# A routed feed-forward layer on one core: the order of slot tiles, routing visits and table payload

## The chip, the cores and the metric

The kernel is one program on one core of a Trainium2 chip. Its time is device microseconds of one launch. Below, TensorE multiplies, VectorE (DVE), ScalarE (ACT) and GpSimd (POOL) compute and copy, and SyncE (SP) issues transfers.

## The reference

`x` has 4 x 1024 tokens of 512 float32 numbers, and each of the 4 batches names one of 64 categories. With `t` = 4096 tokens, 8 experts and room for 512 tokens in each:

```
h = x @ cond_W[cat] + cond_b[cat]                 # conditioning, per batch
probs = softmax(h @ Wr);  eidx = argmax(probs);  p = probs[eidx]
rank = number of earlier tokens with the same eidx
keep = rank < 512;  slot (eidx, rank) gets the token
per expert: y = relu(h[slots] @ W1[e]) @ W2[e] * p        # W1 512x2048, W2 2048x512
out = x + y scattered to its tokens (a dropped token gets x alone)
```

## The kernel before, in words

The program is written by hand, one instruction list per engine. Each engine works its list in order; semaphores tie the lists together. There is no planner: what stands earlier in a list runs earlier.

Matrix products keep float32 accuracy by splitting each operand into a high part (ScalarE copies it to fp32r) and a low part (VectorE subtracts the high part from the raw value), and adding three products, high x high, high x low and low x high.

*Conditioning and routing.* The tokens are 32 tiles of 128, four to a chunk. `cond_tile` multiplies a tile in 12 matmuls of 512 columns into one of three rotating PSUM banks, and VectorE's `store_h` adds the bias, which frees the bank. At the third k-block of a chunk's first tile TensorE waits for the second half of the chunk's low split. Chunks of x and blocks of the conditioning weight are split on ScalarE and VectorE at the tiles that `SPLIT_X` and `SPLIT_W` name; an entry of `SPLIT_X` holds the tiles of a chunk's first and second half. On a batch of eight tiles routing works in visits that TensorE makes between tiles, at tile numbers in lists by batch: `m_turn` (M_TURN: conditioning weight times router weight, by the transposed weight), copied on ScalarE and transposed on VectorE by `copy_m` (M_SUM); `route` (ROUTE: 64 matmuls of 128 columns with a weight of 32 columns: the logits), copied on ScalarE; `choose` on VectorE (CHOOSE: one-hot choice, counts of the tiles before); `rank_of` on TensorE and `place` on VectorE (both at PLACE: probability, its three-part float16 payload, `packed` = one-hot x payload, rank of each token, eight one-hot `select` rows); `fill_table` (FILL: 32 matmuls of packed x select, which add up the slot tables). At one tile the order on TensorE is turn, fill, rank, route; on VectorE store, choose, copy_m, place, splits.

GpSimd stores finished chunks of h to memory (`store_chunk`); the last 8 tiles are stored one by one by SyncE. When the table is complete, `gather_early` fetches rows of expert 0 from memory. Rows of the last 4 tiles (`late`) are added by a one-hot product of three bfloat16 parts. Then the first quarter of expert 0 is multiplied directly, and from there on the loop's scheme holds.

*The experts.* A step is one quarter of one expert: 128 x 4 hidden columns by 512 slots. The first product of a quarter is done by a seven-product scheme (P1 to P7, each two pairs of six matmuls of 256 columns), from sums of blocks of W1 (`sum_w1`: four GpSimd additions) and of x (`sum_x`). The second product (`second_product(i, q, s)`: 12 matmuls of 512 columns for one of four slot tiles s) runs one step behind the first. TensorE's step is: first_and_fifth, slot tile 0, second_and_sixth, slot tile 1, seventh_and_third, slot tile 2, fourth, slot tile 3. ScalarE makes the hidden tiles (`relu`, high part) behind the third and fourth products, VectorE their low parts (`hidden_lo`); slot tile 0 of the next step waits for all four. VectorE also makes low parts of W1, W2 and x, and scales finished outputs (`finish(i, s)`) behind slot tile s of a quarter that ends an expert. Once an expert, four VectorE transposes (`transpose_chunk`) turn the gathered rows between two steps; GpSimd gathers and scatters rows.

The loop covers experts 0 to 6 (28 steps); two steps of the last expert and its last second product follow.

## Time and profile before

| what | value |
|---|---|
| median of 3 runs | 798.09 us (797.9 to 798.27) |
| the profiled execution | 797.76 us, of which span 796.1 us |
| granted TensorE clock, mean | 0.999 of full speed |
| TensorE busy | 789.6 us, 99% of the span |
| VectorE, ScalarE, GpSimd busy | 581.2, 351.8, 517.2 us |
| chain of waits, share of TensorE | 98% |

The span is the time from the first to the last instruction; the profiled execution's own time is 1.7 us longer. Durations are of that one execution. In a timeline a matmul's length has some 0.16 us of latency in it, so lengths overlap; the rate is read from one start to the next. "xN" is a run of N alike.

### The profile page before, as it was taken

The numbers are of one execution on the slowest core, as the hardware profiler recorded it, in microseconds if no ns is written. First come the engines' busy times: TensorE is split into PE (matmuls) and PEld (weight loads), VectorE is DVE, ScalarE is ACT, GpSimd is POOL, SyncE is SP. The second block draws the span as 40 slices with busy tenths as digits, with TensorE's granted clock in tenths as the row PEclk, the third lists the DMA queues.
The fourth block names the chain that finished last, engine by engine and source line by source line (L and its number), as shares of the span: only waits on it lengthen the run. The fifth ranks groups of instructions, "written<-read, shape, count | busy, mean of one in ns | idle before, by whom it ended". The sixth has DMA issues, their size and how long they took to land.

```text
span 796.1 us, 14205 instructions
## 1 busy us (share of the span) xinstructions
PE 789.6 (99%) x5255; PEld 702.3 (88%) x5255; DVE 581.2 (73%) x764; ACT 351.8 (44%) x537; POOL 517.2 (65%) x392
## 2 busy tenths in 40 slices
PE   9999999999999999999999999999999999999997
PEld 6778789899999999999999999999999999999996
DVE  5678969799757886689657965797578767895532
ACT  4322246536443544455444544454445344544420
POOL 1000148898887688768878688768876888663601
PEclk9999999999999999999999999999999999999999
DMA  8988543542554154424553444435441544254201
GB/s 285 376 309 296 205 167 132 185 159 96 170 178 146 54 191 165 163 105 175 170 171 109 168 162 149 154 129 172 172 144 58 185 157 142 103 188 176 71 1 54
DMA packets 61103, 127.20 MB, mean 160 GB/s; under 512 B 8310, under 2 KB 8310, under 8 KB 60562
## 3 DMA queue, kind: packets, MB, share of 16 engines
q1 hardware_dynamic: 47714, 95.19, 34.4%
q0 software_dynamic: 13216, 31.38, 12.2%
q8 instruction: 17, 0.28, 0.1%
q10 hardware_dynamic: 144, 0.26, 0.1%
q14 instruction: 12, 0.10, 0.0%
HBM read 110.13 MB, written 25.17 MB: 170 GB/s over the span
## 4 chain that ended last, share of the span: by engine, by line
PE 98%; DMA 1%; SPq 0%; issue 0%; POOL 0%; DVE 0%; ACT 0%; POOLq 0%
PE y_ps L1500 44%; PE acc_ps L1398 20%; PE tp_ps L1398 19%; PE acc_ps L1316 6%; PE tp_ps L1316 3%; PE tp_ps L1247 1%; PE acc_ps L1412 1%; PE tp_ps L1412 1%; DMA stage<-cond_w 1%; PE y_ps L1232 0%; PE y_ps L1365 0%; PE acc_ps L1297 0%; PE y_ps L1316 0%; PE y_ps L1268 0%; PE y_ps L1374 0%
## 5 line engine op out<-in xcount | busy, mean ns | idle before, releaser
L1500 PE MATMUL y_ps<-w_split,xt_split 128*128 128x512 f32 x1536 | 371.1, 391 | 0.0
L1500 PEld LDWEIGHTS y_ps<-w_split,xt_split 128*128 128x128 f32 x1536 | 280.7, 188 | 53.2
L1398 PE MATMUL acc_ps<-x_split,w_split 128*128 128x256 f32 x1320 | 181.1, 283 | 0.0
L1398 PEld LDWEIGHTS acc_ps<-x_split,w_split 128*128 128x128 f32 x1320 | 172.1, 191 | 5.0 <-DVE w_split L956 0.2
L1398 PE MATMUL tp_ps<-x_split,w_split 128*128 128x256 f32 x1284 | 176.4, 283 | 0.0
L967 DVE TENSOR_TENSOR w_split<-stage,w_split 128x1024 fp32r<-128x1024 f32 x64 | 113.1, 1807 | 80.8 <-ACT w_split L671 80.8
L1398 PEld LDWEIGHTS tp_ps<-x_split,w_split 128*128 128x128 f32 x1284 | 167.6, 191 | 4.9 <-ACT logits_t L730 0.2
L546 POOL DMA_INDIRECT rows<-h_rows,idx_all x112 | 133.7, 1194 | 32.9 <-issue 32.3
L664 ACT ACTIVATE w_split<-stage 128x1024 fp32r<-128x1024 f32 x64 | 54.0, 843 | 97.8 <-PE acc_ps L1398 46.0
L503 POOL TENSOR_TENSOR w_sums<-stage 128x512 f32<-128x512 f32 x31 | 42.9, 1385 | 67.1 <-DVE w_split L956 60.1
L956 DVE TENSOR_TENSOR w_split<-stage,w_split 128x1024 fp32r<-128x1024 f32 x64 | 73.5, 1148 | 15.7 <-ACT w_split L664 15.6
L956 DVE TENSOR_TENSOR w_split<-w_sums,w_split 128x1024 fp32r<-128x1024 f32 x62 | 77.7, 1255 | 5.6 <-ACT w_split L664 5.4
L733 ACT ACTIVATE xt_split<-tp_ps 128x512 fp32r<-128x512 f32 x64 | 38.0, 598 | 79.7 <-PE tp_ps L1398 77.8
L562 POOL DMA_INDIRECT out<-rows,put_all x32 | 37.6, 1176 | 52.4 <-DVE rows L1090 44.9
L733 ACT ACTIVATE xt_split<-acc_ps 128x512 fp32r<-128x512 f32 x64 | 38.0, 598 | 68.9 <-PE acc_ps L1398 67.1
L664 ACT ACTIVATE w_split<-w_sums 128x1024 fp32r<-128x1024 f32 x62 | 65.1, 1049 | 5.4 <-POOL w_sums L506 4.9
L671 ACT ACTIVATE w_split<-stage 128x1024 fp32r<-128x1024 f32 x64 | 64.3, 1060 | 0.0
L1067 DVE SCALAR_TENSOR_TENSOR xt_split<-tp_ps,xt_split 128x512 fp32r<-128x512 f32 x64 | 44.0, 691 | 26.4 <-ACT xt_split L733 25.9
L1067 DVE SCALAR_TENSOR_TENSOR xt_split<-acc_ps,xt_split 128x512 fp32r<-128x512 f32 x64 | 43.8, 687 | 22.5 <-ACT xt_split L733 21.3
L508 POOL TENSOR_TENSOR w_sums<-stage 128x512 f32<-128x512 f32 x31 | 59.8, 1927 | 0.0
L496 POOL DMA_DIRECT2D h_rows<-rows x6 | 4.8, 797 | 80.4 <-DVE rows L867 80.4
L506 POOL TENSOR_TENSOR w_sums<-w_sums,stage 128x512 f32<-128x512 f32 x31 | 53.9, 1738 | 2.4
(183 smaller groups left out, 802.4 us busy)
## 6 DMA issues: line engine op xcount, KB each, us to landing
stage<-w SPq DMA_DIRECT2D x64, 1024.0 KB, 7.3
b_rows<-x SPq DMA_DIRECT2D x8, 1024.0 KB, 9.4
h_rows<-rows POOLq DMA_DIRECT2D x6, 1024.0 KB, 9.1
stage<-cond_wt SPq DMA_DIRECT2D x4, 1024.0 KB
x_more<-x_t SPq DMA_DIRECT2D x4, 1024.0 KB, 9.1
stage<-x_t SPq DMA_DIRECT2D x3, 1024.0 KB, 7.6
stage<-cond_w SPq DMA_DIRECT2D x3, 1024.0 KB, 9.6
h_rows<-rows SPq DMA_DIRECT2D x8, 256.0 KB, 2.4
```

Source lines behind the costliest of these rows:

```text
L506: nc.gpsimd.tensor_tensor(w1_sum(1), w1_sum(0), w1_raw(0, 0, slot), ALU.subtract).then_inc(s_comb, 1)
L508: nc.gpsimd.tensor_tensor(w1_sum(2), w1_raw(0, 0, slot), w1_raw(1, 0, slot), ALU.subtract).then_inc(s_comb, 1)
L546: pool.indirect_dma_start(out=h_quart[:, t * P:(t + 1) * P], out_offset=None, in_=h_parts, in_offset=bass.IndirectOffsetOnAxis(ap=idx_all[ ...
L664: nc.scalar.activation(split_part(w1s, grp, HI), w1_group(grp, slot), ACTF.Copy).then_inc(s_w1hi, 1)
L671: nc.scalar.activation(w2s[:, slot, HI, ks, :], stage[:, 2 + slot, ks, :], ACTF.Copy).then_inc(s_w2hi, 1)
L733: nc.scalar.activation(hts[:, (u % 2) * QF + tile, HI, :], (upper(u) + lower(u))[tile], ACTF.Relu).then_inc(s_hhi, 1)
L956: nc.vector.tensor_tensor(split_part(w1s, grp, LO), w1_group(grp, (u + 1) % 2), split_part(w1s, grp, HI).bitcast(f32), ALU.subtract).then_ ...
L967: nc.vector.tensor_tensor(w2s[:, slot, LO, ks, :], stage[:, 2 + slot, ks, :], w2s[:, slot, HI, ks, :].bitcast(f32), ALU.subtract).then_inc ...
L1067: nc.vector.scalar_tensor_tensor(hts[:, at, LO, :], (upper(u) + lower(u))[tile], 0.0, hts[:, at, HI, :].bitcast(f32), ALU.max, ALU.subtrac ...
L1316: last = nc.tensor.matmul(cond_bank(n), xts[:, c % 4, a, k, t * P:(t + 1) * P], w2s[:, (c // CPB) % 2, w, k, :], start=(k == 0 and (a, w) ...
L1398: last = nc.tensor.matmul(out, w1s[wg][:, w, wb, k, f], xes[xg][:, a, xb, k, :], start=start and k == 0 and (w, a) == (HI, HI), stop=True, ...
L1500: last = nc.tensor.matmul(y_ps[:, s, :], hts[:, (q % 2) * QF + jj, a, s * P:(s + 1) * P], w2s[:, q % 2, w, jj, :], start=(first and jj == ...
```

## The change

Four things. In the loop TensorE does slot tiles 2 and 3 of the second product one after the other, and fourth behind them; VectorE's list in a step is reordered to go with it. The payload and `packed` are made by GpSimd (`pack`) from the probability that VectorE leaves. The tile lists of routing are changed: turn, fill and route stand at seven tiles instead of ten, and copy_m is ahead of choose at one tile. In the head, the second conditioning block's high part is halved between ScalarE and VectorE as the first already was; some loads of SyncE change places; and the first two of the four sums of W1's second quarter are done ahead of the wait for the late parts.

```diff
...
     M_TURN = [4, 8, 13, 18]
-    M_SUM = [5, 10, 13, 18]
-    ROUTE = [6, 11, 15, 20]
-    CHOOSE = [8, 13, 18, 22]
-    PLACE = [10, 15, 20, 24]
+    M_SUM = [5, 9, 14, 19]
+    ROUTE = [8, 13, 18, 20]
+    CHOOSE = [9, 14, 19, 22]
+    PLACE = [11, 16, 21, 24]
     FILL = [13, 18, 23, 27]
...
     KEEP_FIRST = 12
+    HALVED = 2
+    PAY_STEPS = 5
     LATE = 4
...
         rest = sb("rest", [P, TPB], f32)
+        scaled = sb("scaled", [P, TPB], f32)
         payload = sb("payload", [P, NT, Q], f16)
...
         s_oh = sem("onehot_done")
+        s_prob = sem("prob_done")
+        s_pay = sem("payload_steps_done")
+        s_pack = sem("packed_done")
         s_rank = sem("rank_done")
...
 
+            load_cond(2)
             load_next_xt(4)
-            load_cond(2)
             load_next_xt(5)
...
             load_cond_wt(2)
+            sp.wait_ge(s_turn, 3)
+            load_cond_wt(3)
             load_next_xt(6)
...
             load_cond(3)
-            sp.wait_ge(s_turn, 3)
-            load_cond_wt(3)
 
...
             def sum_w1(g):
+                first_sums(g)
+                second_sums(g)
+
+            def first_sums(g):
                 slot = g % 2
...
                                         ).then_inc(s_comb, 1)
+
+            def second_sums(g):
+                slot = g % 2
                 nc.gpsimd.tensor_tensor(w1_sum(2), w1_raw(0, 0, slot), w1_raw(1, 0, slot), ALU.subtract
...
 
+            def pack(b):
+                tiles = slice(TPB * b, TPB * (b + 1))
+                done = PAY_STEPS * b
+                pool.wait_ge(s_mask, 15)
+                pool.wait_ge(s_prob, b + 1)
+                nc.gpsimd.tensor_copy(payload[:, tiles, 1], prob[:, :]).then_inc(s_pay, 1)
+                pool.wait_ge(s_pay, done + 1)
+                nc.gpsimd.tensor_tensor(rest[:, :], prob[:, :], payload[:, tiles, 1], ALU.subtract).then_inc(s_pay, 1)
+                pool.wait_ge(s_pay, done + 2)
+                nc.gpsimd.tensor_scalar(scaled[:, :], rest[:, :], LOWER, None, ALU.mult).then_inc(s_pay, 1)
+                pool.wait_ge(s_pay, done + 3)
+                nc.gpsimd.tensor_copy(payload[:, tiles, 2], scaled[:, :]).then_inc(s_pay, 1)
+                pool.wait_ge(s_pay, done + 4)
+                nc.gpsimd.tensor_tensor(payload[:, tiles, 3], scaled[:, :], payload[:, tiles, 2], ALU.subtract
+                                        ).then_inc(s_pay, 1)
+                pool.wait_ge(s_pay, done + 5)
+                pool.wait_ge(s_oh, b + 1)
+                if b >= 1:
+                    pool.wait_ge(s_tab, b)
+                nc.gpsimd.tensor_tensor(packed[:, :, :, :],
+                                        onehot.unsqueeze(3).to_broadcast([P, TPB, E, Q]),
+                                        payload[:, tiles, :].unsqueeze(2).to_broadcast([P, TPB, E, Q]),
+                                        ALU.mult).then_inc(s_pack, 1)
+
             for c in range(NCH - 2):
+                for b in range(BATCH):
+                    if TPC * c <= PLACE[b] < TPC * (c + 1):
+                        pack(b)
                 store_chunk(c)
+            pack(BATCH - 1)
 
...
             gather_early()
+            first_sums(1)
             pool.wait_ge(s_part[2], LATE)
-            sum_w1(1)
+            second_sums(1)
             pool.wait_ge(s_hlast, 16 * LATE)
...
                     act.wait_ge(s_acc, TPC * CPB * (b - 1))
-                cols = slice(0, CH // 2 if (b, k) == (0, 0) else CH)
+                cols = slice(0, CH // 2 if b == 0 and k < HALVED else CH)
                 nc.scalar.activation(w2s[:, b % 2, HI, k, cols], stage[:, 1, k, cols], ACTF.Copy
...
                     dve.wait_ge(s_rank, b)
+                    dve.wait_ge(s_pack, b)
                 then(nc.vector.tensor_tensor(onehot, score[:, :, :], wide(best[:, :]), ALU.is_equal))
...
                 then(nc.vector.tensor_reduce(total[:, :], expo[:, :, :], AX.X, ALU.add))
-                then(nc.vector.reciprocal(prob[:, :], total[:, :]))
-                then(nc.vector.tensor_copy(payload[:, tiles, 1], prob[:, :]))
-                then(nc.vector.tensor_tensor(rest[:, :], prob[:, :], payload[:, tiles, 1], ALU.subtract))
-                then(nc.vector.tensor_scalar(payload[:, tiles, 2], rest[:, :], LOWER, None, ALU.mult))
-                then(nc.vector.scalar_tensor_tensor(payload[:, tiles, 3], rest[:, :], LOWER, payload[:, tiles, 2],
-                                                    ALU.mult, ALU.subtract))
+                if b >= 1:
+                    dve.wait_ge(s_pay, PAY_STEPS * b)
+                nc.vector.reciprocal(prob[:, :], total[:, :]).then_inc(s_prob, 1)
                 if b >= 1:
                     dve.wait_ge(s_tab, b)
-                nc.vector.tensor_tensor(packed[:, :, :, :],
-                                        onehot.unsqueeze(3).to_broadcast([P, TPB, E, Q]),
-                                        payload[:, tiles, :].unsqueeze(2).to_broadcast([P, TPB, E, Q]),
-                                        ALU.mult)
                 dve.wait_ge(s_rank, b + 1)
...
             dve.wait_ge(s_mask, 15)
-            def first_half():
-                dve.wait_ge(s_w0[0], 16)
-                nc.vector.tensor_copy(w2s[:, 0, HI, 0, CH // 2:], stage[:, 1, 0, CH // 2:]).then_inc(s_whalf, 1)
-                dve.wait_ge(s_whalf, 1)
+            def second_half(k):
+                dve.wait_ge(s_w0[k], 16)
+                nc.vector.tensor_copy(w2s[:, 0, HI, k, CH // 2:], stage[:, 1, k, CH // 2:]).then_inc(s_whalf, 1)
+                dve.wait_ge(s_whalf, k + 1)
 
...
                 split_first(k)
-                if k == 0:
-                    first_half()
+                if k < HALVED:
+                    second_half(k)
                 split_cond(0, k)
...
                 store_h(n // TPC, n % TPC)
+                if n in M_SUM:
+                    copy_m(M_SUM.index(n))
                 if n in CHOOSE:
                     choose(CHOOSE.index(n))
-                if n in M_SUM:
-                    copy_m(M_SUM.index(n))
                 if n in PLACE:
...
                 new, done = u == QN - 1 and not last, u == QN
-                for half in range(2):
-                    split_w2(i, u, half)
+                if not done:
+                    split_w2(i, u, 0)
+                    split_w2(i, u, 1)
                 add_fifths(i, u)
...
                     finish(i, 0)
+                    split_w2(i, u, 0)
                 if not last:
...
                     finish(i, 2)
+                    split_w2(i, u, 1)
+                    finish(i, 3)
                 hidden_lo(i, u, 2)
...
                     split_x(i, 3)
-                if done:
-                    finish(i, 3)
 
...
                 pe.wait_ge(s_sel, b + 1)
+                pe.wait_ge(s_pack, b + 1)
                 for t in range(TPB):
...
                             pe.wait_ge(s_whi, k + 1)
+                            if k < HALVED:
+                                pe.wait_ge(s_whalf, k + 1)
                         elif w == LO:
...
             keep_warm(KEEP_FIRST)
-            pe.wait_ge(s_whalf, 1)
             first_tiles()
...
 
-            def step(i, u):
+            def step(i, u, last=False):
                 first_and_fifth(i, u)
...
                 second_product(i, u - 1, 2)
-                fourth(i, u)
-                second_product(i, u - 1, 3)
+                if last:
+                    fourth(i, u)
+                    second_product(i, u - 1, 3)
+                else:
+                    second_product(i, u - 1, 3)
+                    fourth(i, u)
 
...
             for u in range(2, QN):
-                step(E - 1, u)
+                step(E - 1, u, u == QN - 1)
             for s in range(SB):
...
```

## Rows read from the trace of the kernel before

**Rows 1.** The page, part 1: busy us, share of the span, instructions.
```profile
PE 789.6 (99%) x5255; PEld 702.3 (88%) x5255; DVE 581.2 (73%) x764; ACT 351.8 (44%) x537; POOL 517.2 (65%) x392
```

**Rows 2.** Chain of waits, the loop's last steps: start us, length us, what.
```profile
755.27 1.43 PE tp_ps L1398 x12
756.70 2.75 PE y_ps L1500 x12
759.45 2.87 PE acc_ps L1398 x24
...
777.74 13.64 PE y_ps L1500 x60
```

**Rows 3.** Timeline of TensorE, conditioning stage: start, length, line, names, shape, count.
```profile
29.23 3.01 PE L1316 MATMUL tp_ps<-w_split,xt_split 128*128 128x512 f32 x12
32.08 2.88 PE L1316 MATMUL acc_ps<-w_split,xt_split 128*128 128x512 f32 x12
34.89 1.08 PE L1232 MATMUL y_ps<-stage,wr 128*32 128x128 f32 x32
...
41.54 3.01 PE L1316 MATMUL acc_ps<-w_split,xt_split 128*128 128x512 f32 x12
44.48 1.96 PE L1247 MATMUL tp_ps<-x_more,m 128*32 128x128 f32 x64
...
102.39 5.61 PE L1316 MATMUL acc_ps<-w_split,xt_split 128*128 128x512 f32 x24
107.84 2.89 PE L1316 MATMUL tp_ps<-w_split,xt_split 128*128 128x512 f32 x12
```

**Rows 4.** Timeline of ScalarE, head; in brackets its idle time and the releaser.
```profile
5.37 0.42 ACT L633 ACTIVATE w_split<-stage 128x256 fp32r<-128x256 f32 x1 [0.99 <-DMA stage<-cond_w]
...
8.42 0.63 ACT L633 ACTIVATE w_split<-stage 128x512 fp32r<-128x512 f32 x1 [1.54 <-DMA stage<-cond_w]
```

**Rows 5.** The page, part 6: transfers by line, KB each, us to landing.
```profile
stage<-cond_w SPq DMA_DIRECT2D x3, 1024.0 KB, 9.6
```

**Rows 6.** Timeline of VectorE, routing.
```profile
52.74 0.43 DVE L877 STREAM_TRANSPOSE by_tok<-logits_t 128x256 f32<-128x256 f32 x1
...
55.38 0.31 DVE L856 STREAM_TRANSPOSE m<-m_rows 128x128 f32<-128x128 f32 x1
...
56.54 0.69 DVE L867 TENSOR_TENSOR rows<-acc_ps,b_rows 128x512 f32<-128x512 f32 x1 [0.28 <-PE acc_ps L1316]
57.15 1.22 DVE L837 TENSOR_TENSOR xt_split<-stage,xt_split 128x1024 fp32r<-128x1024 f32 x1
...
77.88 0.18 DVE L907 CAST payload<-prob 128x8 f16<-128x8 f32 x1
...
79.06 0.22 DVE L919 TENSOR_TENSOR ranks<-y_ps,chosen 128x64 f32<-128x64 f32 x1
...
79.57 2.19 DVE L924 TENSOR_SCALAR select<-iota_c,place_all 128x512 f16<-128x512 f16 x8
```

**Rows 7.** Timeline of GpSimd, early gather and sums.
```profile
102.63 1.10 POOL L532 DMA_INDIRECT early_rows<-h_rows,tok_all  x1 [11.30 <-DMA h_rows<-rows]
...
118.57 1.76 POOL L511 TENSOR_TENSOR w_sums<-stage,w_sums 128x512 f32<-128x512 f32 x1
```

**Rows 8.** Timeline of VectorE, splits of the first hidden input.
```profile
119.09 1.78 DVE L1050 TENSOR_TENSOR x_split<-turned,x_split 128x512 fp32r<-128x512 f32 x1
```

**Rows 9.** Timeline of TensorE, end of the first quarter and one loop step.
```profile
127.56 3.33 PE L1398 MATMUL acc_ps<-x_split,w_split 128*128 128x256 f32 x24
...
254.32 3.04 PE L1398 MATMUL acc_ps<-x_split,w_split 128*128 128x256 f32 x24
```

**Rows 10.** Timeline of VectorE, around two step ends of the loop.
```profile
253.70 4.13 DVE L1073 STREAM_TRANSPOSE turned<-rows 128x512 f32<-128x512 f32 x4
...
272.73 1.41 DVE L1067 SCALAR_TENSOR_TENSOR xt_split<-acc_ps,xt_split 128x512 fp32r<-128x512 f32 x2
...
280.15 4.48 DVE L967 TENSOR_TENSOR w_split<-stage,w_split 128x1024 fp32r<-128x1024 f32 x2
```

## The prediction

> **What bounds the kernel now.** I read the page's engine table first, then the chain of waits, then each engine's timeline. The table has TensorE busy for 99% of the span [rows 1], and its chain is 98% TensorE. So only two things move the time: a change in how long TensorE's own stream lasts, and a wait put into it or taken out. An edit on VectorE, ScalarE or GpSimd counts only where TensorE waits for it.
>
> In the loop over experts a step is seven groups of twelve narrow matmuls (256 columns) and four of twelve wide ones (512). The chain has them end to end: 1.43 us for twelve narrow and 2.87 for 24 behind wide ones, 2.75 for twelve wide between narrow ones [rows 2]. Four times 2.75 and seven times 1.435 are the 21.04 us of a step; nothing is left for waits. The sixty wide ones at the end take 13.64, or 2.73 a dozen, so an entry into a wide group costs 0.02 and one into a narrow group gives 0.01 back.
>
> In the conditioning stage two tiles without a visit take 5.45 (102.39 to 107.84) [rows 3], 2.725 each. A tile behind a routing visit takes 2.85, one ahead of a visit 2.81 (29.23, 32.08, 34.89): a visit costs 0.12 + 0.09 = 0.21 beside its own matmuls. Between the rank matmuls and route(1) the tile takes 2.94 (41.54 to 44.48), so a rank visit of its own costs about 0.13.
>
> **The sum, part by part** (us, minus is faster).
>
> *Halved second block.* ScalarE's 0.63 us split of the second conditioning block starts when the load lands, and TensorE waits for it [rows 4]. Half the columns take 0.42 (at 5.37) and save 0.21; VectorE, idle there, does the rest. **-0.2** (-0.3 to +0.1, if VectorE gets there last).
>
> *Visits.* Turn, route and fill stand at 4, 6, 8, 11, 13, 15, 18, 20, 23, 27 now and at 4, 8, 13, 18, 20, 23, 27 afterwards: three fewer, 3 x 0.21 = 0.63. Turn(1) is no longer alone and ranks no longer precede a route (about 0.3 less), while ranks alone go from two tiles to four (2 x 0.13 more). **-0.65** (-0.3 to -0.9). Turn(1) now comes at about 32.5 instead of 34.89 and needs a load issued at 21.8, just behind the wait for turn(0); a load of that kind lands 9.6 after issue [rows 5], at 31.4, so I take nothing and keep +0.4 as a bound. SyncE issues cond_w(2) before x_t(4) now, which does not wait for route(0); the third turning load and x_t(6), x_t(7), cond_w(3) go out together near 50 to 55 and four of them need some 12 us, so cond_w(3) lands near 65. ScalarE waits for it at tile 16 and VectorE's stores are some tiles behind, but TensorE needs that weight only at tile 24: nothing.
>
> *The second half of chunk 4.* Its low split stays at tile 14, and choose(1) now comes to tile 14 too, ahead of it on VectorE. Count from the start of tile 14: its end 2.85, the store starts 0.2 behind, 0.61 to the next instruction (56.54 to 57.15) [rows 6], copy_m(2) 0.24, choose 2.64 (52.74 to 55.38), the split 1.22: done at 7.8. TensorE is through tile 15 at 5.58 and asks for that half after six matmuls of tile 16, at 6.94. Before, choose was at tile 13 and the split done four tiles' time earlier. **+0.9** (0 to +1.0). This wait eats the visits' gain.
>
> *Choosing and placing later, payload on GpSimd.* The payload instructions leave VectorE: 1.18 us a batch (77.88 to 79.06), so place is 3.1 instead of 4.3 with its eight selects of 2.1 together. GpSimd gets five chained small instructions and one of 256 elements; its nearest row is 1.3 to 1.8 for 512 elements [rows 7], so I estimate 2.3 a batch, bounds 1.5 to 5. It starts when prob is there, 1.3 us behind the rank tile, and fill comes 5.6 us behind it: 4.3 us of cover. GpSimd has nothing else then but storing a chunk; chunk 2's store goes 3 to 4 us later, and VectorE needs its buffer 14 us later. At 5 us a fill would wait 0.7 twice. For batch 3 VectorE is tight: from the end of tile 21 store, place(2), both splits of chunk 6, store and choose(3) are 0.2 + 0.6 + 3.1 + 2.3 + 0.6 + 2.4 = 9.2; TensorE reaches rank(3) after 9.1. **+0.2** (0 to +1.3). From there VectorE runs about 2 us behind its old times, into tile 27.
>
> For the upper bound the row is this: a 512-element VectorE split with both inputs in SBUF took 1.78 at 119.09 [rows 8] and ended 0.5 us behind GpSimd's sum that began at 118.57, where the same form takes 0.69 otherwise. The Trainium skill ("SBUF — State Buffer", Who interferes with whom) has it that such an instruction, or a VectorE one in a two-port mode, and a GpSimd instruction lock each other out for a whole instruction. By that rule pack and the selects would block each other, up to an instruction's length, and rank(3) would come later by that much; the trace agrees for the sums (1.78 against 0.69), and no row of before shows GpSimd beside the selects.
>
> *Early rows.* The gather waits for tile 27's row store to land: its first issue is at 102.63 [rows 7]. Tile 27's store on VectorE is some 1.8 us late, so the gather is at 104.5. TensorE arrives at 111.0; the third of four gathers lands at 111 to 112 and is asked for at 111.9. **+0.1** (0 to +1.0).
>
> *First two sums of W1(1) ahead of the wait.* They now run beside VectorE's last remainders, which set the end of the late rows; one blocked instruction there is up to 0.7. **+0.2** (0 to +0.8). In return, of the four sums beside the first x splits only two are left, and the blocked 1.8 us (the 1.78 row, and one of 1.39 before it) goes. TensorE's first 24 narrow matmuls in that stretch took 3.33 where 24 take 2.87 [rows 2, 9], and some 0.3 more is lost beside them; a wait for the copies of the new pair, 0.2, is next. **-0.5** (-0.7 to 0).
>
> *Loop.* Slot tiles 2 and 3 side by side, and fourth beside the next step's first group, remove one wide and one narrow entry a step: 0.02 - 0.01 = 0.015, for 29 steps **-0.4** (-0.5 to 0). The Trainium skill ("TensorE: Matmul & The Clock Gate", Back-to-back issue gap) gives the isolated gap as a function of the columns alone; by that this edit is worth nothing, and the sum comes out 0.4 higher. The trace differs by the 0.02 above.
>
> What it costs: fourth now ends with the step, and the next product's slot 0 needs hidden tile 3, which was 5.6 us behind fourth and is now 2.9. In the step that starts at 254.32 [rows 9] fourth ends at 272.6; VectorE's pair of hidden tiles, 1.41 us, starts at 272.73 and is done at 274.14 [rows 10]. Shifted by the 2.7 of the product that went ahead, it is done 1.5 us into the next step: 1.3 to spare. finish(3) and the split of W2 are moved so that VectorE is free by then. **0**.
>
> Sum: -0.2 - 0.65 + 0.9 + 0.2 + 0.1 + 0.2 - 0.5 - 0.4 = **-0.35**. The profiled execution took 797.76 (span 796.1, 1.7 around it), so it would take 797.4. The median of the runs is 0.33 above it: **797.8**.
>
> **Rivals.**
> A, slower: *the transposes come late.* Once an expert, four transposes (4.13 at 253.70) follow the last W1 split of a step, which now ends 2.7 later. They then run from 2.1 to 6.3 us into the step; two W2 splits follow, 3.5 to 4.5 us (the latter is the 4.48 row), then an addition of 0.4 that the seventh product wants at 11.25. That is 10.2 to 11.2 against 11.25. GpSimd's x sums run beside it as well; if they block VectorE for one more instruction (1.1 us, the 1.78 row), TensorE waits up to 1 us in seven experts, and knock-on waits for sums and copies come on top: about 0.4 a time is 2.8, 800.6. It decides from a pair of splits above 4.5 us. Against it: such a pair takes at most 4.48 in the trace.
> B, faster: *the wait at tile 16 is not there or hides another.* The sum without it is -1.25; with all small costs at nothing, -1.75: 796.3 to 796.8. For it: little but my counting of one VectorE queue, with 0.9 of 7.8 us over.
> C: *GpSimd and VectorE block each other in routing.* Rank(3), the table and the early gather each late by most of their bounds: +1.5 on the sum, 799.3.
> D: *the adjacency gives nothing* and visits half: about +0.7, 798.5; still no measurable change.
>
> **How the numbers follow.** A measurement of this kernel tells some 0.2%, 1.6 us, from no change: 796.5 to 799.7. Forecast (with D) 0.60, A 0.12, B 0.16, C 0.12. A is slower, C a third of its cases, B nearly all faster than the bound or at it. That makes 0.17 faster, 0.65 same, 0.18 slower. The range takes the forecast's own bounds and half of A, B and C: 796.3 to 799.9.
>
> **What would show it.** A gap in TensorE's stream of 0.7 to 1.0 at tile 16 behind six matmuls, released by VectorE's split of chunk 4, and choose(1) just ahead of that split; seven clusters of small matmuls in place of ten; steps of 21.02 instead of 21.04, with 24 wide in 5.47; the first narrow matmuls behind the first quarter with at most 0.3 of gaps; the early gather's first issue near 104.5. The forecast fails if steps of the loop are longer than 21.04, if a fill waits for pack, or if tile 16 starts clean.

## The result, and the profile after

The changed kernel took 801.94 us in the median of 6 runs (801.63 to 803.34), against 798.12 for the kernel before (6 runs, 797.9 to 798.28). The ratio is 1.0054 [1.0044, 1.0064]: half a percent slower, and outside the predicted range of 796.3 to 799.9. The profiled execution took 801.63 us, 3.87 more than the one before; its span is 799.7. Two of the six, at 803.12 and 803.34, had a mean granted clock of 0.996 where the other four had 0.999, and took 1.4 more than these. Neither was profiled, so no row shows where the clock fell.

The page's engine table (busy us, share, instructions), which answers to [rows 1]:

```profile
PE 789.6 (99%) x5255; PEld 702.5 (88%) x5255; DVE 586.7 (73%) x745; ACT 350.3 (44%) x537; POOL 539.7 (67%) x416
```

TensorE's busy time is what it was. All 3.6 us of the longer span are gaps. The chain of waits says that they aren't in the loop (start us, length us, what), answering to [rows 2]:

```profile
142.59 10.91 PE y_ps L1540 x48
...
756.17 5.47 PE y_ps L1540 x24
763.07 2.88 PE acc_ps L1438 x24
...
781.37 13.64 PE y_ps L1540 x60
```

The 24 wide matmuls stand side by side. The x48 piece is the end of the first quarter's stretch and the start of the steady loop; x60 is its end. They lie 638.78 us apart, and 639.36 in the trace before, where x48 starts at 138.38: the loop gained 0.58. x48 itself starts 4.21 later. TensorE's timeline shows why (start, length, engine, line, operation, count; in brackets idle time and releaser):

```profile
60.41 1.67 PE L1357 MATMUL tp_ps<-w_split,xt_split 128*128 128x512 f32 x6 [0.67 <-DVE xt_split L879]
...
87.53 3.04 PE L1357 MATMUL acc_ps<-w_split,xt_split 128*128 128x512 f32 x12
90.78 0.20 PE L1295 MATMUL y_ps<-chosen,before 128*128 128x64 bf16 x1 [0.21 <-DVE prior L939]
...
99.70 0.63 PE L1307 MATMUL y_ps<-select,packed 128*32 128x128 f16 x32 [0.41 <-DVE select L960]
...
102.31 0.33 PE L1319 MATMUL y_ps<-ident,slots 128*128 128x128 f32 x1 [0.98 <-ACT slots L694]
...
104.56 6.00 PE L1357 MATMUL acc_ps<-w_split,xt_split 128*128 128x512 f32 x24
...
113.12 1.72 PE L1414 MATMUL y_ps<-ident,early_rows 128*128 128x128 f32 x12
...
118.93 1.30 PE L1405 MATMUL y_ps<-late_sel,late_parts 128*128 128x128 bf16 x18 [1.47 <-DVE late_parts L986]
120.07 0.26 PE L1367 MATMUL tp_ps<-tok_n,spread_w 128*128 128x32 f16 x4
...
131.83 3.04 PE L1438 MATMUL acc_ps<-x_split,w_split 128*128 128x256 f32 x24
```

Five waits in brackets, and 24 matmuls that take 6.00, where the kernel before had no wait between the head and the first quarter. With the same points read from the trace before, the loss adds up (us; a wait costs its idle time and 0.1 to 0.5 more):

| point | before | after | later by | lost since the point above |
|---|---|---|---|---|
| tile 4 (end of the head) | 17.49 | 17.37 | -0.12 | -0.12 |
| tile 24 | 87.52 | 87.53 | 0.01 | +0.13: the wait at tile 16, less what the visits save |
| fill(3) | 98.84 | 99.70 | 0.86 | +0.85: ranks of batch 3, last selects |
| the table's matmul | 100.20 | 102.31 | 2.11 | +1.25: slots |
| early rows | 110.56 | 113.12 | 2.56 | +0.45: 24 matmuls of tiles 29 and 30 in 6.00, before 5.61 [rows 3] |
| spread | 115.62 | 120.07 | 4.45 | +1.89: late parts |
| x48 | 138.38 | 142.59 | 4.21 | -0.24: 3.04 for the 3.33 of [rows 9] |
| x60 | 777.74 | 781.37 | 3.63 | -0.58: the loop |

Who holds up VectorE stands in the timelines of GpSimd and of VectorE, after (GpSimd first):

```profile
91.94 0.81 POOL L502 DMA_DIRECT2D h_rows<-rows  x1 [7.08 <-DVE rows L909]
95.02 0.19 POOL L544 CAST payload<-prob 128x8 f16<-128x8 f32 x1 [2.26 <-DVE prob L951]
...
96.62 0.62 POOL L558 TENSOR_TENSOR packed<-chosen,payload 128x256 f16<-128x256 bf16 x1
97.17 1.81 POOL L609 MEMSET early_rows<- 128x2048 f32 x1
106.38 1.15 POOL L573 DMA_INDIRECT early_rows<-h_rows,tok_all  x1 [7.40 <-DMA h_rows<-rows]
...
111.77 1.29 POOL L513 TENSOR_TENSOR w_sums<-stage 128x512 f32<-128x512 f32 x1
113.14 1.62 POOL L516 TENSOR_TENSOR w_sums<-w_sums,stage 128x512 f32<-128x512 f32 x1
```

```profile
95.27 4.38 DVE L960 TENSOR_SCALAR select<-iota_c,place_all 128x512 f16<-128x512 f16 x8
...
111.20 2.42 DVE L986 TENSOR_TENSOR late_parts<-late_rest,late_parts 128x512 bf16<-128x512 f32 x1
113.54 1.77 DVE L980 TENSOR_TENSOR late_rest<-rows,late_parts 128x512 f32<-128x512 f32 x1
```

And one row of GpSimd's timeline in the kernel before that the prediction did not use:

```profile
89.51 1.83 POOL L568 MEMSET early_rows<- 128x2048 f32 x1
```

GpSimd clears the buffer of the early rows with one instruction. Before, it did so at 89.51, four microseconds ahead of the last selects. In the changed list this instruction stands behind `pack(BATCH - 1)`, which waits for a probability until 95.02. So it now runs beside the selects: they take 4.38 where [rows 6] has 2.19. Fill and the table wait for the selects, the stores of the last tiles follow, and the early gather leaves at 106.38 instead of 102.63 [rows 7]. GpSimd's next items, the two sums that the change moved ahead of the wait, start only at 111.77, exactly beside the last late parts, and hold two VectorE instructions of 0.69 for 2.42 and 1.77. TensorE waits for those.

For the 0.4 lost in tiles 29 and 30 the profile names no releaser, but TensorE's list does. Between the two tiles it waits for `s_win` and reads four addresses into registers (lines 1394 and 1395 of the kernel after). VectorE signals `s_win` when it has written `window_at`, a few instructions behind the copy of the table. From the timelines of VectorE and of TensorE's weight loads (PEld), before:

```profile
101.37 0.16 DVE L932 CAST window_at<-window 1x4 int32<-1x4 f32 x1
102.16 5.41 PEld L1316 LDWEIGHTS acc_ps<-w_split,xt_split 128*128 128x128 f32 x24
```

and after:

```profile
104.19 0.16 DVE L968 CAST window_at<-window 1x4 int32<-1x4 f32 x1
104.33 2.69 PEld L1357 LDWEIGHTS acc_ps<-w_split,xt_split 128*128 128x128 f32 x12
107.52 2.61 PEld L1357 LDWEIGHTS acc_ps<-w_split,xt_split 128*128 128x128 f32 x12 [0.51 <-issue]
```

Before, `window_at` is there 0.63 ahead of tile 29's first weight load, and tile 30 follows without a gap. After, it comes only with that load. The 14 traces of this document fall into the same two groups: 0.63 or 0.64 ahead in five, and 5.61 for the two tiles; with the load or later in nine, and 0.4 to 0.7 lost up to the early rows. No run changes this wait alone, so the cause is argued from the list and the traces, not shown.

### The profile page after: what moved, and what is told of

Same layout as the page of the kernel before. It is cut to its first block, busy times and chain, and to the rows that moved or that the text cites. A ratio compares the mean times of both kernels' runs of the same rounds, so it can differ in the third digit from the quotient of the medians.

```text
span 799.7 us, 14227 instructions
## 1 busy us (share of the span) xinstructions
PE 789.6 (99%) x5255; PEld 702.5 (88%) x5255; DVE 586.7 (73%) x745; ACT 350.3 (44%) x537; POOL 539.7 (67%) x416
## 4 chain that ended last, share of the span: by engine, by line
PE 95%; DVE 3%; issue 2%; ACT 0%; POOL 0%; POOLq 0%
PE y_ps L1540 44%; PE acc_ps L1438 20%; PE tp_ps L1438 19%; PE acc_ps L1357 5%; PE tp_ps L1357 2%; PE tp_ps L1285 1%; PE acc_ps L1452 1%; PE tp_ps L1452 1%; PE acc_ps L1375 1%; PE acc_ps L1338 1%; PE y_ps L1270 0%; DVE late_parts L986 0%; DVE xt_split L879 0%; PE y_ps L1357 0%; DVE select L960 0%
## 5 line engine op out<-in xcount | busy, mean ns | idle before, releaser
L1540 PE MATMUL y_ps<-w_split,xt_split 128*128 128x512 f32 x1536 | 365.6, 391 | 0.0
L587 POOL DMA_INDIRECT rows<-h_rows,idx_all x112 | 137.7, 1229 | 33.0 <-issue 32.1
L1003 DVE TENSOR_TENSOR w_split<-stage,w_split 128x1024 fp32r<-128x1024 f32 x64 | 101.1, 1610 | 44.4 <-ACT w_split L713 44.4
L992 DVE TENSOR_TENSOR w_split<-w_sums,w_split 128x1024 fp32r<-128x1024 f32 x62 | 96.3, 1555 | 2.8 <-ACT w_split L706 2.8
L992 DVE TENSOR_TENSOR w_split<-stage,w_split 128x1024 fp32r<-128x1024 f32 x64 | 76.7, 1199 | 6.6 <-ACT w_split L706 6.4
L603 POOL DMA_INDIRECT out<-rows,put_all x32 | 42.8, 1336 | 51.7 <-DVE rows L1126 44.2
L513 POOL TENSOR_TENSOR w_sums<-stage 128x512 f32<-128x512 f32 x31 | 43.5, 1402 | 36.7 <-DVE w_split L992 36.3
L524 POOL TENSOR_TENSOR w_sums<-stage,w_sums 128x512 f32<-128x512 f32 x31 | 55.6, 1794 | 0.0
L521 POOL TENSOR_TENSOR w_sums<-stage 128x512 f32<-128x512 f32 x31 | 50.9, 1643 | 4.0 <-DVE late_parts L986 4.0
L516 POOL TENSOR_TENSOR w_sums<-w_sums,stage 128x512 f32<-128x512 f32 x31 | 51.7, 1669 | 2.4
```

The source lines that it names most:

```text
L516: nc.gpsimd.tensor_tensor(w1_sum(1), w1_sum(0), w1_raw(0, 0, slot), ALU.subtract).then_inc(s_comb, 1)
L524: nc.gpsimd.tensor_tensor(w1_sum(3), w1_raw(0, 1, slot), w1_sum(1), ALU.subtract).then_inc(s_comb, 1)
L587: pool.indirect_dma_start(out=h_quart[:, t * P:(t + 1) * P], out_offset=None, in_=h_parts, in_offset=bass.IndirectOffsetOnAxis(ap=idx_all[ ...
L992: nc.vector.tensor_tensor(split_part(w1s, grp, LO), w1_group(grp, (u + 1) % 2), split_part(w1s, grp, HI).bitcast(f32), ALU.subtract).then_ ...
L1003: nc.vector.tensor_tensor(w2s[:, slot, LO, ks, :], stage[:, 2 + slot, ks, :], w2s[:, slot, HI, ks, :].bitcast(f32), ALU.subtract).then_inc ...
L1540: last = nc.tensor.matmul(y_ps[:, s, :], hts[:, (q % 2) * QF + jj, a, s * P:(s + 1) * P], w2s[:, q % 2, w, jj, :], start=(first and jj == ...
```

## The experiments

My theory after this reading: two collisions on GpSimd, of about 1.7 us each, are nearly all of the miss, and payload on GpSimd as such is harmless. The rivals: the payload's own instructions are what costs, or the later tiles. In the expectations a run goes by its label: e1 to e7 are experiments 1 to 7, and e9 to e13 are experiments 8 to 12.

How the results are read: where TensorE reaches tile 4 differs from one execution to the next (17.27 to 18.66 over these traces, by when loads land). So beside the times each trace is given by its **middle**, from the start of tile 4 to the start of x48. It is 120.89 before and 125.22 after. It is read from one trace of each kernel, but stretches that two kernels have in common agree well: from tile 4 to tile 24 it is 70.14 to 70.16 in the kernel after and in experiments 1 to 3. The loop, x48 to x60, is 638.78 in each kernel that has the new order and 639.35 or 639.36 in each that hasn't.

**1. The clearing ahead of pack(3)** (after, otherwise unchanged).

```diff
+            pool.wait_ge(s_acc, NT - 8)
+            nc.gpsimd.memset(early_rows[:, :, :], 0.0).then_inc(s_zero, 1)
             pack(BATCH - 1)
-            pool.wait_ge(s_acc, NT - 8)
-            nc.gpsimd.memset(early_rows[:, :, :], 0.0).then_inc(s_zero, 1)
```

> The changed kernel with GpSimd's clearing of early_rows put ahead of pack(3) instead of behind it. Theory L (lock): the clearing, 1.81 us beside the last eight selects, blocks VectorE, which makes them 4.38 instead of 2.65. Moved away, the selects are back at 2.6 to 2.9, the waits of the last fill (0.41) and of the table (0.98) nearly go, the early gather starts near 104.6 instead of 106.4, and the time falls by 1.8 to 2.8, to 799.2 to 800.2. Theory Q (queue): VectorE is late by its order alone (two splits and place at tile 21), the clearing is a bystander; the selects stay above 4 and the time stays within 0.4 of 801.9.

The profiled execution took 800.01, 1.62 less than after's; middle 123.48, 1.74 less. The median of four is 801.33 (1.0043 [1.0026, 1.006]), outside the expected 799.2 to 800.2: the three other executions (800.83 to 801.94) had a granted clock of 0.996, as two of after's had. So by its times alone this run is weak. Experiments 2 and 3 differ by the same edit, over ten executions each with no clock under 0.998, and there it is worth 1.83 (800.01 to 798.18). From its timelines:

```profile
92.86 1.83 POOL L569 MEMSET early_rows<- 128x2048 f32 x1
```

```profile
95.36 2.66 DVE L960 TENSOR_SCALAR select<-iota_c,place_all 128x512 f16<-128x512 f16 x8
```

The waits of fill and table are gone. The selects take 2.66 beside pack and 2.19 without it, so pack costs them 0.47. The wait for the late parts remains whole.

**2. The two sums back behind the wait** (after, otherwise unchanged).

```diff
             gather_early()
-            first_sums(1)
             pool.wait_ge(s_part[2], LATE)
+            first_sums(1)
             second_sums(1)
```

> The changed kernel with the first two W1(1) sums of GpSimd back behind the wait for the late parts. Theory L: those two sums (1.29 and 1.62) block two VectorE instructions of the late rows (2.42 and 1.77 instead of 0.69 each); behind the wait both are 0.69, TensorE's wait of 1.47 for the late parts falls under 0.3, but the first x splits are blocked again (1.4 and 1.8 us instead of 0.7) and some 0.4 of waits returns near the first quarter's end: net 0.8 to 1.4 faster, 800.5 to 801.1. Theory Q: the late rows are late because tiles 27 to 30 are; the wait stays above 1 and the time within 0.4 of 801.9, or is slower by what the early sums gave.

800.01 (799.6 to 800.36, 10 runs), 1.0025 [1.0015, 1.0035]; middle 123.55, 1.67 less than after. Late parts take 0.69 each and TensorE's last wait is gone. The time is below the expected 800.5 to 801.1: up to the spread matmuls the edit gains 1.97, more than the wait of 1.47 shows, and 0.3 of it is lost again behind them. The selects' 4.39 and the waits at fill and table stay.

**3. Both.**

> Both edits, clearing ahead of pack(3) and all four sums behind the wait. Theory L: the two collisions were all of the excess over the forecast; left are the wait at tile 16 (0.7), rank(3) (0.2) and the gain of the loop and of the visits: 797.8 to 798.6. Theory Q: no better than 801.3.

798.18 (797.58 to 799.1, 10 runs), 1.0004 [0.9994, 1.0014]: no difference from before that can be told. The middle is 121.80, 3.42 less than after, and 1.74 + 1.67 is 3.41: the two collisions are independent and add up. What is left of waits in brackets behind the head are tile 16 and rank(3); tiles 29 and 30 still take 6.01.

**4. The loop's new order alone** (the kernel before with the change's edits of `step` and of VectorE's list in the loop).

```diff
+                if last:
+                    fourth(i, u)
+                    second_product(i, u - 1, 3)
+                else:
+                    second_product(i, u - 1, 3)
+                    fourth(i, u)
```

> The kernel before with the loop's part of the change alone: slot tiles 2 and 3 side by side, fourth last, VectorE's step reordered. By the chain, steps of 21.02 instead of 21.04, 29 of them, no waits: 0.4 to 0.7 faster than before, 797.4 to 797.7. If the reordered step only pays because the head runs late, or if rival A (late transposes) holds from this starting point, no gain or slower, 798.1 and up.

797.58 (796.98 to 798.3, 10 runs), 0.9995 [0.9985, 1.0005]. The time alone can't tell it from nothing; the trace can: loop 638.78 instead of 639.36, middle 120.87 as before.

**5. Experiment 3 with the second half of chunk 4 split a tile earlier.**

```diff
-    SPLIT_X = [None, None, (3, 4), (6, 7), (12, 14), (16, 17), (21, 21), (23, 25)]
+    SPLIT_X = [None, None, (3, 4), (6, 7), (12, 13), (16, 17), (21, 21), (23, 25)]
```

> The kernel of e3 (clearing first, sums behind) with chunk 4's second split at tile 13 instead of 14, ahead of choose(1). Theory: the wait at tile 16 (0.67 after six matmuls, 0.83 with what lies around it) goes and nothing later takes it, so TensorE is 0.8 earlier to the end: 797.3 to 797.5 where e3 took 798.2. Rival: VectorE's queue at tiles 21 to 24 is the bound there (rank(3) waits 0.2 for it already) and does not move with TensorE, so the gain is given back and the time stays at 798.1.

797.46 (796.65 to 798.07, 11 runs), 0.9992 [0.9983, 1.0001]; middle 120.83, 0.97 less than experiment 3. The wait at tile 16, shown as 0.67, is gone. It was one VectorE queue that was too long, by 0.7 as shown, where the prediction had counted 0.9.

**6. Payload and packed back on VectorE** (after, otherwise unchanged; `packed` signals `s_pack`, and the calls of `pack` are gone from GpSimd's list).

```diff
-                nc.vector.reciprocal(prob[:, :], total[:, :]).then_inc(s_prob, 1)
+                then(nc.vector.reciprocal(prob[:, :], total[:, :]))
+                then(nc.vector.tensor_copy(payload[:, tiles, 1], prob[:, :]))
...
+                nc.vector.tensor_tensor(packed[:, :, :, :],
...
+                                        ALU.mult).then_inc(s_pack, 1)
```

> The changed kernel with the payload and packed back on VectorE; tile lists, loop and early sums as changed. Theory L: GpSimd has no pack, so it clears early_rows near 92 to 94, and the selects are 2.19 instead of 2.65 to 4.38. VectorE gives 1.2 a batch for the payload and gets 0.5 (for the last batch 2.2) back; rank(3) waits 0.7 to 1.0 instead of 0.2 (its own 1.2 less 0.5), the last fill not more than that; the sums still block the late rows. 800.6 to 801.5 against 801.9. If the payload's own cover was worth its place: slower than 801.9.

801.49 (801.32 to 801.67, 4 runs), 1.0045 [1.003, 1.006]; middle 125.35, against 125.22. The clearing is ahead of the selects again (93.59) and they take 2.19, but VectorE's own 1.2 us a batch make rank(3) wait 1.03 and the table 0.71, and the collision with the sums is as it was (2.36 and 1.77). Taking the payload away from GpSimd doesn't save the kernel: it swaps one lateness for another. The middles differ by 0.13; by the times the two can't be told apart.

**7. The clearing beside the selects, in the kernel before.** This isolates the collision: one more wait holds GpSimd's clearing until the ranks of batch 3 are made. VectorE signals `s_ranks` ahead of its selects.

```diff
             pool.wait_ge(s_acc, NT - 8)
+            pool.wait_ge(s_ranks, BATCH)
             nc.gpsimd.memset(early_rows[:, :, :], 0.0).then_inc(s_zero, 1)
```

> The kernel before, with one thing changed: GpSimd's clearing waits until the last ranks are read, so it runs beside VectorE's last eight selects. Theory L: the selects take 3.8 to 4.0 instead of 2.19. VectorE has some slack here, since the last fill came 3.3 behind them: that fill does not wait; chunk 7's second split and tile 27's store come up to 1.7 later, the table may wait up to 0.3. Time 798.0 to 798.8. Theory Q (write-only clearing does not block VectorE): selects at 2.19 and the time of before, 797.9.

From the timelines of GpSimd and of VectorE:

```profile
93.94 1.81 POOL L570 MEMSET early_rows<- 128x2048 f32 x1 [4.05 <-DVEq L924]
```

```profile
93.90 3.83 DVE L927 TENSOR_SCALAR select<-iota_c,place_all 128x512 f16<-128x512 f16 x8
```

The selects take 1.64 longer beside a clearing of 1.81, with no pack in this kernel. TensorE has most of the slack here, though: no wait in brackets, 798.4 (798.25 to 798.81, 10 runs), 1.0007 [0.9997, 1.0016]; the middle is 121.27. Its 0.38 more is all in tiles 29 and 30, which take 5.99: `window_at` is late again. In the changed kernel the slack was already used up by the later tiles, so there the same collision cost 1.7. The Trainium skill ("SBUF — State Buffer", Who interferes with whom) says that a VectorE instruction in a two-port mode, which it lists `tensor_scalar` as able to enter, and one of GpSimd exclude each other for the whole instruction. Only for a VectorE instruction with two inputs in SBUF does it limit this to GpSimd instructions that read SBUF. 3.83 against 2.19 beside a clearing, which reads nothing, agrees; in which mode the selects run no view shows.

**8. Experiment 5 with chunk 6 split at tile 20**, ahead of place(2), so that VectorE is at choose(3) sooner.

```diff
-    SPLIT_X = [None, None, (3, 4), (6, 7), (12, 13), (16, 17), (21, 21), (23, 25)]
+    SPLIT_X = [None, None, (3, 4), (6, 7), (12, 13), (16, 17), (20, 20), (23, 25)]
```

> e5 with both splits of chunk 6 at tile 20 instead of 21, where VectorE idled 2.8 before tile 21's store. Theory: choose(3) comes 1.1 earlier, the 0.2 wait at rank(3) goes, VectorE is 1.1 ahead into tile 27, the early gather too: 0.2 faster than e5, 797.1 to 797.3. Rival: ScalarE's copy of the logits and its splits come too late at tile 20 and delay tile 21's store and place(2): the wait moves to a fill, and the time is that of e5 or up to 0.5 above.

796.49 (796.07 to 796.87, 11 runs), 0.9982 [0.9973, 0.9991]: the best version, and the interval is clear of the kernel before. The middle is 120.08, 0.75 less than experiment 5's; 0.38 more of the difference in span is the head. TensorE's timeline no longer has a wait behind its first matmul, and tiles 29 and 30 are back at 5.61:

```profile
101.35 5.61 PE L1357 MATMUL acc_ps<-w_split,xt_split 128*128 128x512 f32 x24
...
126.51 3.34 PE L1438 MATMUL acc_ps<-x_split,w_split 128*128 128x256 f32 x24
```

I had expected the rank wait of 0.2 alone to go, and 797.1 to 797.3. That wait was worth 0.36; the other 0.38 is in tiles 29 and 30, where `window_at` is 0.63 ahead again. The 3.34, for after's 3.04, is what the sums' return behind the wait gave back.

**9. The two sums in GpSimd's idle time before the gather** (experiment 8, the first two sums behind a wait for the copy of the slots).

```diff
+            pool.wait_ge(s_slots, 1)
+            first_sums(1)
             pool.wait_ge(s_zero, 1)
...
-            first_sums(1)
             second_sums(1)
```

> e9 with the first two W1(1) sums put where GpSimd waits for tile 27's row store: behind the copy of the slot tables (near 99.8), ahead of the early gather (102.5). Theory L: there VectorE has mostly PSUM reads; two of its instructions are blocked by up to 1 us, the early gather may be 0.3 late; the late rows stay at 0.69 each, and of the four sums beside the first x splits two are left, which takes back the 0.4 to 0.7 lost behind the first quarter (3.33 for 24 narrow becomes 2.9 to 3.0): 795.8 to 796.3. Rival: the block falls on tile 27's store and the table, so the gather starts 1 us later and TensorE waits for late or early rows: 796.5 to 797.3.

From the timelines of GpSimd, VectorE and TensorE:

```profile
99.62 1.29 POOL L513 TENSOR_TENSOR w_sums<-stage 128x512 f32<-128x512 f32 x1 [3.74 <-ACT slots L695]
100.99 1.29 POOL L516 TENSOR_TENSOR w_sums<-w_sums,stage 128x512 f32<-128x512 f32 x1
103.31 1.17 POOL L575 DMA_INDIRECT early_rows<-h_rows,tok_all  x1 [1.02 <-DMA h_rows<-rows]
```

```profile
101.03 1.30 DVE L1013 TENSOR_SCALAR tok_all<-tok_n 128x32 uint32<-128x32 f16 x1
102.42 0.16 DVE L969 CAST window_at<-window 1x4 int32<-1x4 f32 x1
```

```profile
105.45 3.01 PE L1358 MATMUL acc_ps<-w_split,xt_split 128*128 128x512 f32 x12 [0.42 <-issue]
```

797.13 (796.66 to 797.76, 11 runs), 0.9988 [0.9979, 0.9997]; middle 120.52, 0.44 more than experiment 8. Late parts are clean, and the x splits are too (24 narrow in 3.04 again), but the second sum now holds `tok_all`, one small VectorE instruction, for 1.30 instead of 0.18 (the stores take their usual 0.68). `window_at` stands behind it and comes 0.66 later than tile 29's first weight load, and tile 30 waits 0.42. The expectation was missed; the collision moved rather than went.

**10. The two sums ahead of the wait, in the kernel before.**

> The kernel before with one thing changed: the first two W1(1) sums ahead of the wait for the late parts. GpSimd is through the early gather at 107.7 there, so the sums run to about 110.6, when VectorE has a late part and a remainder of tile 30 and is past them before tile 31's store. Theory L with the position deciding: one instruction blocked, at most 0.3 on the late rows, and 0.5 gained behind the first quarter: 797.4 to 797.8. Rival: the early sums cost their collision wherever the gather ends, 1 us or more: 798.8 to 799.3.

From the timelines of GpSimd, VectorE and TensorE:

```profile
109.64 1.63 POOL L510 TENSOR_TENSOR w_sums<-w_sums,stage 128x512 f32<-128x512 f32 x1
```

```profile
109.18 0.93 DVE L958 TENSOR_TENSOR late_parts<-late_rest,late_parts 128x512 bf16<-128x512 f32 x1
110.04 1.78 DVE L952 TENSOR_TENSOR late_rest<-rows,late_parts 128x512 f32<-128x512 f32 x1
```

```profile
115.44 1.23 PE L1373 MATMUL y_ps<-late_sel,late_parts 128*128 128x128 bf16 x18 [0.53 <-DVE late_parts L958]
```

798.39 (798.19 to 799.18, 10 runs), 1.0004 [0.9995, 1.0014], between the two expectations. The middle is 121.58, 0.69 more than before, but most of that is not the edit's: 0.44 is lost ahead of tile 24, long before the sums, nearly all of it at the first route visit, where TensorE waits for a transposition that came late behind a load. From tile 24 to x48 it is 51.11 instead of 50.86, 0.25 more. So even with the gather on time this edit costs a little more (a TensorE wait of 0.53) than it gains. With the gather 3.7 late it costs 1.67 (experiment 2), with the gather 2.1 late 1.68 (experiment 1 against 3).

**11. Experiment 8 without the head's halving** (`HALVED = 1`).

> e9 with only the first conditioning block halved, as before. Theory: the second block's copy is 0.63 instead of 0.42 and TensorE waits for it: 0.2 slower than e9, 796.7. Rival: how late the block lands differs from execution to execution by more (TensorE's wait for it was 0.3, 0.6 and 1.1 in three traces with the same head), so nothing can be told: 796.3 to 796.7.

796.69 (796.38 to 797.54, 11 runs), 0.9982 [0.9973, 0.9991]; middle 120.06. In its trace tile 4 starts at 18.66, but that varies between 17.27 and 18.07 in nine traces with the halving and between 17.49 and 18.66 in five without. By the ratios to the kernel before, 0.9982 in both experiments, it is worth nothing that can be told. (Of the three waits that the expectation names, the 1.1 is experiment 4's and its head isn't halved.)

**12. Experiment 8 with payload and packed on VectorE.**

> e9 with the payload and packed on VectorE. Theory: with the collisions gone the question is only VectorE's own time: it does 1.18 more a batch and gets 0.46 back from the selects, so it is 0.7 later at rank(3), where e9 had some 0.9 to spare, and 1.4 later at tile 27; the early gather starts near 103.9: 0 to 0.5 slower than e9, 796.5 to 797.0. Rival: the payload on GpSimd is worth a microsecond by itself: 797.5.

797.95 (797.3 to 798.4, 11 runs), 0.9997 [0.9988, 1.0006]; middle 121.51, 1.43 more than experiment 8. From the timelines of TensorE and of VectorE:

```profile
86.95 0.63 PE L1310 MATMUL y_ps<-select,packed 128*32 128x128 f16 x32 [0.61 <-DVE select L963]
...
100.55 0.33 PE L1322 MATMUL y_ps<-ident,slots 128*128 128x128 f32 x1 [0.20 <-ACT slots L690]
```

```profile
95.69 2.19 DVE L963 TENSOR_SCALAR select<-iota_c,place_all 128x512 f16<-128x512 f16 x8
```

Both expectations were too low. Of the 1.43, 0.68 is lost ahead of tile 24, at the fill of batch 2, and some 0.4 each at the table and at tile 30 (5.98 for the two tiles). Payload on GpSimd, which the bare result seems to condemn, is worth about 1.4 us once the clearing is ahead of it; by the two ratios, 0.9997 and 0.9982, it is 1.2.

## Why the prediction was wrong

**The step that failed** is the term "choosing and placing later, payload on GpSimd, +0.2". It rested on the sentence "GpSimd has nothing else then but storing a chunk". That was true of the first three batches only. Behind pack(3), in unchanged lines of GpSimd's list, stood the clearing of the early rows. [rows 7] points at it: the 11.30 of idle time ahead of the early gather begin at 91.33, so GpSimd had worked until then, on the clearing. I had asked what pack itself costs and whom its result keeps waiting, not what is queued behind the instruction that waits. Rival C named the mechanism, GpSimd and VectorE blocking each other in routing, and the consequences (rank(3), table and early gather late), but priced it at +1.5 in all, from the bounds of terms that knew of pack alone. With a 1.8 us instruction in it this collision by itself was 1.74 (experiment 1); experiment 7 shows it without pack, as 1.64 on the selects.

**The second mis-sized term** is "first two sums ahead of the wait, +0.2 (0 to +0.8)". Taking it out gained 1.67 (experiment 2), and that is net of the 0.3 which the edit had gained behind it. I allowed for one blocked instruction of up to 0.7. There were two, lengthened by 1.73 and 1.08, and they were exposed because the gather, which is ahead of the sums in GpSimd's list, was late. This is no consequence of the first collision: with that one gone and the gather near its forecast time the sums still cost 1.68 (experiment 1 against 3), while in the kernel before, with the gather on time, they cost 0.25 net (experiment 10). The prediction had the later gather in one term and did not carry it into this one. "In return -0.5" came as -0.24 to -0.3: 24 narrow matmuls took 3.04 instead of 3.33, and nothing more.

**The early gather**: forecast 104.5, first issue at 106.38; with the clearing out of the way 104.77 (experiment 1). The forecast held for the kernel that I thought I had.

**What came as written.** The loop gained 0.58, forecast 0.4 (0 to 0.5), a little beyond its bound: steps of 21.02, wide pairs of 5.47, no wait, so rival A fell, and D too. (The working writes 0.02 - 0.01 as 0.015; measured is 0.02 a step.) Tile 16 waits behind six matmuls for the low split of chunk 4, with choose(1) just ahead of it (0.97 when removed, forecast 0.9); rival B fell. That and the visits nearly cancel: tile 24 starts at 87.53 and 87.52, so the visits gained 0.84, forecast 0.65. Pack takes 2.2 us from 95.02 to 97.24, forecast 2.3, and no fill waits for `packed`. Rank(3) waits 0.21, forecast 0.1 from 9.2 against 9.1 us.

**The sum once more**: with both collisions taken out, experiment 3, the terms still in the kernel add up, without the head's, to -0.65 + 0.9 + 0.2 + 0.1 - 0.4 = +0.15. Its middle and loop together are 121.80 + 638.78 = 760.58, and 760.25 before: +0.33. That the rest came out within 0.2 is in part luck, as errors of both signs cancel: the visits and the loop gained some 0.2 each more than forecast, rank(3) and what follows it cost some 0.2 more, and the 0.4 of tiles 29 and 30 was in no term. The whole miss of the span up to x60, 3.63 against the forecast -0.35, is 3.98: 1.74 for the clearing, 1.97 for the sums (net +1.67, where the terms +0.2 and -0.5 make -0.3), 0.18 for the rest and 0.08 for the head, forecast -0.2 and measured -0.12.

**Open**: whether it is the wait for `s_win` that tile 30 loses 0.4 to, as the traces suggest; and where the granted clock falls in the executions at 0.996. The latter was seen only in the kernel after and in experiment 1, never in a profiled execution.

## What to carry to other kernels

When work that waits is inserted into an engine's list, read the whole list behind it, unchanged lines too, and ask for each item when it ran before, what it will now run beside, and whether one can hold up the other; an item that was harmless because it was early is the one to look for. When work goes to GpSimd, see that its big instructions miss VectorE's critical ones: here the same move gained 0.1 us by the middle with a clearing behind it (experiment 6) and 1.4 us with it ahead (experiment 12). Before dropping a change with several parts, take the parts that its trace blames out one by one. That alone only came back to the kernel before (experiment 3); with two splits moved a tile or so earlier as well, the version that kept the rest took 796.49 against 797.83, 0.2% less (experiment 8).

## What the runs showed of the hardware

- An instruction of GpSimd that only writes (clearing 128 x 2048, 1.81 us) holds VectorE's float16 selects: eight took 3.83 in place of 2.19 in experiment 7.
- A VectorE instruction with two inputs in SBUF that was held by a GpSimd sum ended 0.55 us behind the sum's end each time: 113.62 against 113.06 and 115.31 against 114.76 in the kernel after, 110.11 against 109.56 and 111.82 against 111.27 in experiment 10. [rows 7, 8] have 120.87 against 120.33. The first of these five began 0.57 before the sum did (111.20 and 111.77) and was held all the same; by the starts in the timeline alone one can't tell who waits.
- A small VectorE instruction is held too: `tok_all` of 128 x 32, with one input, took 1.30 in place of 0.18 in experiment 9 and ended with the sum.
- GpSimd's small chained instructions (8 elements) took 0.19 to 0.38 us, one every 0.3 to 0.45, and the broadcast product of 256 elements 0.62. The whole pack, chain and product, made the eight selects beside it 0.47 longer (experiments 1 and 8, against 12).
- A wait costs TensorE more than the idle time in brackets: 0.97 for the 0.67 at tile 16, 0.36 for the 0.20 at rank(3), 1.25 for the 0.98 at the table, 1.97 for the 1.47 at the late parts.
